# Contiguous 32-column blocks for the VectorE transposes and 32-partition transfers, in a batched matrix product on one Trainium2 core

## The reference, cut to what matters

```python
# x: (8, 512, 512) float32, itok: (8,) int32 with values 1 to 98, T: (100, 512, 512) float32
def reference(x, itok, T):
    Tb = T[itok - 1]                              # one 512x512 matrix for each batch
    return x + jnp.einsum('bij,bjk->bik', Tb, x)  # 8 products of 512x512 by 512x512
```

## Time and profile before

| what | us |
|---|---|
| median of 3 runs | 103.46 |
| lowest and highest of the 3 | 102.8, 105.82 |
| the profiled execution | 102.88 |
| its span | 101.1 |
| TensorE busy in the span (matmuls) | 95.7 |
| VectorE busy | 87.0 |
| GpSimd busy | 73.1 |
| ScalarE busy | 65.4 |

### The profile page before, as it was taken

How to read it: one execution, slowest core, us unless ns; L and a number is a source line. 1 busy time by engine, 2 the same in 40 slices (tenths; PEclk the granted TensorE clock), 3 DMA queues, 4 the chain that set the end, 5 groups by cost and what they waited for, 6 DMA issues and landing times.

```text
span 101.1 us, 1833 instructions
## 1 busy us (share of the span) xinstructions
PE 95.7 (95%) x440; PEld 79.2 (78%) x440; DVE 87.0 (86%) x101; ACT 65.4 (65%) x87; POOL 73.1 (72%) x38
## 2 busy tenths in 40 slices
PE   3999999999999999999999999999999999999950
PEld 3996888888888888887887888888888888888840
DVE  0168889999999999989999999999999999993250
ACT  0957598858585969677676767696867768462100
POOL 2004199999979797978989898989797989908100
PEclk9999999999999999999999999999999999999998
DMA  2899798889999879999999999999999782505074
GB/s 58 288 309 389 191 276 221 257 237 333 302 305 282 264 173 341 252 274 325 246 348 285 319 221 351 217 313 288 284 321 283 250 302 67 211 0 207 6 286 129
DMA packets 22125, 25.30 MB, mean 250 GB/s; under 512 B 2402, under 2 KB 16994, under 8 KB 22114
## 3 DMA queue, kind: packets, MB, share of 16 engines
q10 hardware_dynamic: 4850, 15.34, 47.6%
q1 hardware_dynamic: 17264, 9.84, 36.6%
HBM read 16.78 MB, written 8.39 MB: 249 GB/s over the span
## 4 chain that ended last, share of the span: by engine, by line
PE 87%; DMA 5%; SPq 3%; issue 0%; DVE 0%
PE same L470 29%; PE same L459 28%; PE diff L481 28%; DMA T_sb<-T 5%; SPq L170 2%; PE turned L444 2%; SPq L155 1%; PE diff L491 1%; PE same L491 0%; DVE out_sb L415 0%
## 5 line engine op out<-in xcount | busy, mean ns | idle before, releaser
L302 POOL TENSOR_TENSOR xL<-x_sb,xH 128x1024 fp32r<-128x1024 f32 x14 | 33.8, 2416 | 6.2 <-ACT xH L211 6.1
L318 POOL TENSOR_TENSOR TD_r<-TH_r,TL 128x1024 fp32r<-128x1024 f32 x14 | 33.9, 2420 | 4.1 <-issue 3.7
L470 PE MATMUL same<-xL,TL 128*128 128x512 f32 x128 | 34.6, 392 | 0.0
L459 PE MATMUL same<-xH,TH_r 128*128 128x512 f32 x128 | 34.4, 391 | 0.0
L481 PE MATMUL diff<-xD,TD_r 128*128 128x512 f32 x124 | 33.2, 390 | 0.0
L247 ACT ACTIVATE diff<-same 128x512 f32<-128x512 f32 x31 | 18.1, 583 | 22.4 <-PE same L470 15.8
L358 DVE STREAM_TRANSPOSE turned<-T_sb 128x512 f32<-128x512 f32 x28 | 29.7, 1110 | 0.6 <-DMA T_sb<-T 0.4
L459 PEld LDWEIGHTS same<-xH,TH_r 128*128 128x128 f32 x128 | 23.9, 188 | 5.4 <-ACT TH_r L225 0.3
L470 PEld LDWEIGHTS same<-xL,TL 128*128 128x128 f32 x128 | 23.7, 188 | 5.2 <-DVE TL L380 0.3
L481 PEld LDWEIGHTS diff<-xD,TD_r 128*128 128x128 f32 x124 | 23.3, 188 | 4.9
L388 DVE TENSOR_TENSOR out_sb<-x_sb,diff 128x512 f32<-128x512 f32 x31 | 21.5, 693 | 3.9 <-PE diff L481 3.9
(11 more groups left out here) (29 smaller groups left out, 21.0 us busy)
## 6 DMA issues: line engine op xcount, KB each, us to landing
out<-out_sb ACTq DMA_DIRECT2D x15, 512.0 KB, 6.3
T_sb<-T SPq DMA_DIRECT2D x112, 64.0 KB, 4.9
x_sb<-x ACTq DMA_DIRECT2D x13, 512.0 KB, 5.9
x_sb<-x SPq DMA_DIRECT2D x2, 512.0 KB, 6.0
x_sb<-x ACTq DMA_DIRECT2D x2, 256.0 KB, 2.8
T_sb<-T SPq DMA_DIRECT2D x2, 256.0 KB, 4.7
T_sb<-T SPq DMA_DIRECT2D x1, 512.0 KB, 6.3
out<-out_sb SPq DMA_DIRECT2D x1, 256.0 KB, 2.6
```

The costliest lines, as they stand in the source:

```text
L302: nc.gpsimd.tensor_tensor(half(xL, h), x_sb[b % X_SLOTS][:, i:i + 2], half(xH, h).bitcast(fp32), ALU.subtract).then_inc(xL_ready, 2)
L318: nc.gpsimd.tensor_tensor(TD_r[s][:], TH_r[s][:].bitcast(fp32), TL[s][:].bitcast(fp32), ALU.subtract).then_inc(TD_ready, 2)
L459: nc.tensor.matmul(same[U % 2][:], TH_r[p][:, i, j], xH[s][:, j], start=(j == 0), stop=False)
L470: done = nc.tensor.matmul(same[U % 2][:], TL[p][:, i, j], xL[s][:, j], start=False, stop=(j == N - 1))
```

## The change

It concerns batches 2 to 6 (QUADS), and the engine that loads x.

- **Numbering.** In batches 2 to 6 row 128g + 32u + c of x and of the output lies on partition 32g + c, place u. A group of 32 partitions thus holds 128 consecutive rows. One batch of x now comes in four transfers of 32 partitions, 256 KB each, in runs of 2 KB, and one batch of output leaves in four such transfers (`store_quad`). Batches 0, 1 and 7 keep their numbering; batch 7's x is one transfer of 1 MB.
- **T.** The rows of T are numbered to match. In batches 3 to 6 (WHOLE) all of T comes in 4 transfers of 256 KB in place of 16 of 64 KB, still in runs of 512 bytes, and every unit of the batch waits for all four. Batch 2 keeps 16 transfers in the new numbering, batches 1 and 7 keep the old 16.
- **turn.** In batches 2 to 6 the 32 columns of a block are adjacent (step 1, before: step 4).
- **Queues.** x of batches 2 to 7 is loaded by SP, ahead of the same batch's T, and no longer by ScalarE. From batch 4 on SP waits ahead of it for the sums of batch b-4.
- **Stores.** Of batches 2 to 5 ScalarE issues two of the four transfers at the end of iteration 2b+2 and two at the end of 2b+3; of batch 6 all four at the end of iteration 14. In the kernel before, the two halves of a batch were issued at the ends of iterations 2b+1 and 2b+2.

```diff
+    QUADS = range(2, B - 1)
+    WHOLE = range(3, B - 1)
...
+    x_quad = x.rearrange("b (g u c) k -> b g c u k", u=N, c=Q)
+    out_quad = out.rearrange("b (g u c) k -> b g c u k", u=N, c=Q)
...
+    T_quad = T.rearrange("t (m n q) (g c) -> t n g q m c", n=N, q=Q, g=G)
+    T_whole = T.rearrange("t (s q) (g c) -> t g q s c", q=Q, g=G)
...
-        def load_x_half(eng, h):
...
+        def load_x(eng, b):
+            if b not in QUADS:
+                eng.dma_start(x_sb[b % X_SLOTS][:], x_part[b]).then_inc(x_loaded[b % X_SLOTS], 16)
+                return
+            for g in [0, 2, 1, 3]:
+                eng.dma_start(x_sb[b % X_SLOTS][g * Q:(g + 1) * Q], x_quad[b, g]).then_inc(x_loaded[b % X_SLOTS], 16)
...
+                if b in WHOLE:
+                    for g in [0, 2, 1, 3]:
+                        eng.dma_start(T_sb[s][g * Q:(g + 1) * Q].rearrange("q a d -> q (a d)").rearrange("q (s c) -> q s c", c=P),
+                                      T_whole[bass.ds(t, 1), g].rearrange("a q s c -> (a q) s c")).then_inc(T_loaded[s][n], 16)
+                    continue
...
+        def store_quad(eng, b, g):
+            eng.dma_start(out_quad[b, g], out_sb[b % OUT_SLOTS][g * Q:(g + 1) * Q]).then_inc(stored[b % OUT_SLOTS], 16)
...
-            load_T(sp, matrix(itok_sb[0:1, 2:3]), 2)
-            for b in range(T_SLOTS, B):
+            for b in range(2, B):
+                if b >= X_SLOTS:
+                    sp.wait_ge(sum_ready, (b - X_SLOTS + 1) * N)
+                load_x(sp, b)
                 t = matrix(itok_sb[0:1, b:b + 1])
-                wait_turned(sp, (b - T_SLOTS + 1) * N)
+                if b >= T_SLOTS:
+                    wait_turned(sp, (b - T_SLOTS + 1) * N)
                 load_T(sp, t, b)
...
-                if k + 4 < 2 * B:
-                    if b >= 2:
-                        act.wait_ge(sum_ready, (b - 1) * N)
-                    load_x_half(act, k + 4)
...
+                b = (k - 2) // 2
+                if b in QUADS and (k % 2 == 0 or b < B - 2):
+                    act.wait_ge(sum_ready, (b + 1) * N)
+                    for g in [0, 2, 1, 3] if b == B - 2 else [0, 2] if k % 2 == 0 else [1, 3]:
+                        store_quad(act, b, g)
...
+                if b in QUADS:
+                    blocks = T_view(b % T_SLOTS)[:, n].rearrange("p m (u c) -> p m u c", c=Q)
+                else:
+                    blocks = T_sb[b % T_SLOTS][:, n].rearrange("p (m c u) -> p m u c", c=Q, u=N)
```

More of the change, by code:

```diff
@@ L72, in cond_resid @@
         itok_loaded = sem("itok_loaded")
-        half_x_loaded = [[sem(f"half_x_loaded{s}_{i}") for i in range(2)] for s in range(X_SLOTS)]
+        half_x_loaded = [sem(f"half_x_loaded{i}") for i in range(2)]
+        x_loaded = [sem(f"x_loaded{s}") for s in range(X_SLOTS)]
         first_x_loaded = [sem(f"first_x_loaded{i}") for i in range(len(FIRST_X))]
@@ L130, in T_transfers, with x_transfers, stores @@
                 return {0: (1, 1), 1: (2, 1), 2: (N, 1)}
+            if b in WHOLE:
+                return {0: (N, G)}
             return {n: (n + 1, G) for n in range(N)}
+        def x_transfers(b):
+            return G if b in QUADS else 1
+        def stores(b):
+            return G if b in QUADS else 2
         def wait_T_loaded(eng, U):
@@ L157, in load_T @@
                     continue
+                if b in WHOLE:
+                    for g in [0, 2, 1, 3]:
[3 more added lines that the diff above has]
+                if b in QUADS:
+                    for g in [0, 2, 1, 3]:
+                        eng.dma_start(T_view(s)[g * Q:(g + 1) * Q, n],
+                                      T_quad[bass.ds(t, 1), n, g].rearrange("a q m c -> (a q) m c")).then_inc(T_loaded[s][n], 16)
+                    continue
                 for g in range(G):
@@ L177, in _ @@
             load_T(sp, t, 0)
-            load_x_half(sp, 2)
+            load_second_x(sp, 0)
             sp.wait_ge(itok_loaded, 16)
@@ L194, in _ @@
             for s in range(OUT_SLOTS):
-                sp.wait_ge(stored[s], 32 * ((B - 2 - s) // OUT_SLOTS + 1))
+                sp.wait_ge(stored[s], 16 * sum(stores(c) for c in range(s, B - 1, OUT_SLOTS)))
         @block.scalar
@@ L204, in cut_x_half @@
                 b = h // 2
-                act.wait_ge(half_x_loaded[b % X_SLOTS][h % 2], 16 * (b // X_SLOTS + (1 if b % X_SLOTS else 0)))
+                if b == 1:
+                    act.wait_ge(half_x_loaded[h % 2], 16)
+                else:
+                    act.wait_ge(x_loaded[b % X_SLOTS], 16 * sum(x_transfers(c) for c in range(2, b + 1) if c % X_SLOTS == b % X_SLOTS))
                 if b >= X_SETS:
@@ L282, in _ @@
                     copy_xH_half(h)
-                if k < PAIRS - 1:
+                b = (k - 1) // 2
+                if b not in QUADS and b < B - 1:
                     act.wait_ge(sum_ready, 2 * k)
-                    store(act, (k - 1) // 2, slice(2, N) if k % 2 == 0 else slice(0, 2), stored[(k - 1) // 2 % OUT_SLOTS])
+                    store(act, b, slice(2, N) if k % 2 == 0 else slice(0, 2), stored[b % OUT_SLOTS])
+                b = (k - 2) // 2
[3 more added lines that the diff above has]
+                        store_quad(act, b, g)
             act.wait_ge(sum_ready, (B - 1) * N + 2)
@@ L386, in sum_up @@
                 if n == 0 and b >= OUT_SLOTS:
-                    dve.wait_ge(stored[b % OUT_SLOTS], 32 * (b // OUT_SLOTS))
+                    dve.wait_ge(stored[b % OUT_SLOTS], 16 * sum(stores(c) for c in range(b % OUT_SLOTS, b, OUT_SLOTS)))
                 nc.vector.tensor_tensor(out_sb[b % OUT_SLOTS][:, n], x_sb[b % X_SLOTS][:, n], diff[U % 2][:],
```

17 lines of the change are left out of this document (8 added, 9 removed).

## The result

The changed kernel takes 108.43 us (median of 6 runs, 107.52 to 109.21), the kernel before 103.49 in its 6 runs (102.8 to 105.82). The profiled execution took 108.34 us with a span of 106.6, 5.5 us more than the 101.1 of before. I had forecast 102.9, in a range that ended at 105.4.

What follows compares the result with a forecast made beforehand. TensorE was taken as the bound, with VectorE a second bound just keeping up. From 102.88 us, 0.27 was taken off for better supply and 0.3 added for SP's start, giving 102.9 us; range 102.1 to 105.4.

Steps and rivals of the forecast that it cites:

- What bounds the kernel before: TensorE bounds, VectorE just keeps up, T arrives just in time; better supply of TensorE can give back 0.27 us.
- The turn: Batches 2 to 6: step 1 makes a turn 693 instead of 1110 ns, giving VectorE 0.83 us slack a round.
- Fewer transfers of T: From batch 3 on, four issues for sixteen free at least 5.8 us of SP a batch; part of the 0.27 us.
- SP's queue at the start: x of batch 3, behind T pieces, lands at 31.6 to 38.0; stall 0 to 4.6 us, taken as 0.3.
- The bytes speak for the lower end: Bytes from 16 us to the last x of batch 3 take 15.7 us at 268 GB/s, so landing at 31.7.
- Stores: Second pair of quarter stores lands 0.4 us late in each of four batches; VectorE's 0.83 us a round hides it.
- Rival C: 32-partition transfers of x and output cost the DMA engines what T's do: slower, 105.3 us; chance 0.15.
- Its signs: Chain through DMA or VectorE after 35 us, x landings over 6 us, sum_up waiting for stores, DMA share 1 below 270 GB/s.
- the 17 of the estimate: By the 218 GB/s rule a batch needs 14.4 us: 102.9 + 5 x 3.5, up to 120; small part of 0.15.
- A: Full gain, x and T of batch 3 come in time: 102.6 us; chance 0.25.
- B: The turn stays at 1110 ns: 102.9 us if transfers are early, 104.2 with the stores; chance 0.10.
- D: Clearly faster, if untouched runs usually carry more stalls than the profiled one: 101.5 to 102.5 us; chance 0.05.

Runs made afterwards that it cites:

- e4: The kernel before with only the turn's step changed from 4 to 1, all transfers as before: 103.3 us, ratio 0.999.
- e7: The changed kernel with all four stores of batches 2 to 5 issued at the end of iteration 2b+2: 106.41 us, ratio 1.0186.
- e2: The changed kernel with x and stores of batches 2 to 6 and T of batches 3 to 6 spanning 128 partitions: 105.85 us, ratio 1.0173.
- e6: The changed kernel with x, stores and T of batches 2 to 6 over 128 partitions, T of batch 2 also in four transfers: 103.84 us, ratio 1.0017.
- e9: Separate kernel that only moves data, each transfer shape alone: x loads 346 GB/s over 128 partitions, 231 and 235 over 32, 316 on two queues.
- e11: The changed kernel with the turn's step 4 put back in batches 2 to 6, all transfers as changed: 110.38 us, ratio 1.0693.
- e12: The kernel before with T of batches 3 to 6 in four 256 KB transfers over 32 partitions, each unit waiting for all: 106.68 us, ratio 1.026.
- e5: The changed kernel with T of batch 2 also in four 256 KB transfers over 32 partitions instead of 16 pieces: 107.36 us, ratio 1.0311.
- e8: The changed kernel with x loaded by ScalarE again, in halves over 128 partitions: 107.65 us, ratio 1.0277.
- e1: The changed kernel with x of batches 2 to 6 in four transfers over all 128 partitions: 107.21 us, ratio 1.0378.
- e3: The changed kernel with x of batch 3 issued between the second and third unit of T of batch 2: 106.54 us, ratio 1.0293.

## Why the prediction was wrong, step by step

- **What bounds the kernel before** was right: TensorE, with 0.27 us to be had at most. e4 agrees: 9.2 us less of VectorE moved nothing.
- **The turn** was right. By the means, the 20 turns of batches 2 to 6 take (28 x 813 − 8 x 1110) / 20 = 694 ns; I had taken 693. The Trainium skill's rule of 16-byte lines (SBUF — State Buffer, section Door 1: The DMA port swizzle) agrees with this in kind: one instruction, two steps, 1110 and 712 ns (e4). The slack showed before TL, which waited for TH_r, and not before `sum_up`, where I had looked for it.
- **Fewer transfers of T**: the wait of turns for T fell to 0.2 us, as said. "From about 35 us on, x and T of a batch are issued over 10 us ahead" failed: four issues of SP took 6.58 us from 41.21, and T of batches 3 to 6 took 9.2 us to land.
- **SP's queue at the start**: place, issue clock and landing window were right (issued 30.65, landed 35.9, both inside), the choice in it wrong, and this is the first step that failed. "The bytes speak for the lower end": I divided 4.2 MB by 268 GB/s and so took 0.3 us of a 0 to 4.6 us stall. It was 2.06. The rate was near: 264. But by 35.9 us it was 5.25 MB (264 x 19.9) that had moved. I had counted two stores, and there were three; what was left of T of batch 1 at 16 us, and T of batch 3 beside x of batch 3, I had not counted. And bytes could not set this time: SP issued the last of x at 30.2, and my own landing times of 3 to 5.9 us put it at 33 to 36.
- **What a stall costs** I took as its length. In the profiled execution the clock fell behind it, and 1.69 us more went there. No term of the sum or end of the range had it.
- **Stores**: the 5.9 us against 6.3 named the right transfer and the right wait. The landing took 8.55 us, not 6.3, a time that I had carried over from another shape, size and neighbours; the slack of 0.83 us a round hid only part, and 1.48 us reached TensorE. With all four stores issued together, no sum waited (e7). That SP has nothing left to load after 66 us was wrong too: before, it issued T until 82.6 us, and in the changed kernel until 77.9.
- **Rival C** was the larger part of the case, and that the sum has no term for the 32-partition shape is the second and main step that failed: it cost 3.0 us (e2 and e6). Its signs all came: landings of 7.0 and 9.2 us, a sum that waits for a store, a chain through DMA, a DMA share of 1.13 at 261 GB/s. Its price per MB was near: 3.76 us per MB for q1 before, 61.0% x 106.6 / 16.13 = 4.03 after. I halved its 4.7 us, gave it a chance of 0.15 and ended the range at 105.4. My 105.3 for it is 102.9 and that half alone; with the upper half of the stall, which the text names, it would have been 102.6 + 2.35 + 2.3 = 107.3 at least. Against it I set the 310 GB/s of half a microsecond; those were many 64 KB pieces of four groups for an instant, with other transfers beside them, and no measure of what a row of 256 KB transfers holds. e9 measured that at 222 to 235. The second counter, that x's runs of 2 KB would save it, fell too: 346 against 231 GB/s with equal runs.
- **The Trainium skill's rule** (SBUF — State Buffer, section Door 1: The DMA port swizzle) that I argued away, 8 of the 16 ports for 32 adjacent partitions and 218 GB/s at best, spoke against this change and was right in kind. The runs put a little more beside it: 222 to 235 GB/s for one queue of loads (e9). Stores reach 278. That two transfers at once don't combine is what the same page says in another section, "Can I just issue two DMAs to hit both halves?"; here they did combine, with each queue on its own half of the partitions (316), and the measurement decides. Why the loss was 5 us and not the 17 of the estimate, no run shows by itself; these higher rates point that way.

The rivals A, B and D fell: no full gain, no turn of 1110 ns, nothing faster.

## What to carry to other kernels

Before you change the shape of a transfer, divide the bytes of a round by its time, and compare with the rate which that shape reaches in a long row by itself; a rate, or a landing time, read while other shapes were in flight does not carry over. A DMA share near 1 does not say which of the two it is: here it stood at 0.98 with 346 GB/s and at 1.07 with 231. Slack won on an engine that doesn't bound was worth nothing in the kernel before (e4), and about 2 us where data came late (e11). Fewer, larger transfers have two sides: where every unit waits for all four they cost 2.7 us (e12), and where 16 small ones stood ahead of the next batch's x they gave 1.6 back (e5, e6). And when you weigh a stall by bytes over a rate, ask first when its transfer can be issued at all.

## What the runs showed of the hardware that I had not expected

- 256 KB loads in runs of 2 KB, one behind another on one queue: 346 GB/s over 128 partitions, 231 and 235 over 32, whichever order the groups of partitions come in. On two queues, each with its own half of the partitions, 316. Stores: 367 and 278.
- Transfers under way can hold up the engine that issues: four issues of SP took 1.85 us at 28.80, and 6.58 at 41.21 with eight of its transfers not yet landed.
- In the profiled executions, after a single gap of TensorE of 1.89 us (the changed kernel), 1.97 (e7), 2.34 (e11) and 2.73 (e8), about 3.4 us at the 1.2 GHz level followed; with single gaps of 0.92 (e1), 1.07 (e2), 1.13 (e3) and 1.56 us (e5) the granted clock of the stretch behind stayed 1.00. The price was 1.7 us, nearly as much as the stall itself.
